# Delta attention of a four-layer block: large matrix products cut into parts between runs of small ones, token factors formed earlier, key norms by batch on column tiles of 32 tokens

## The reference

```python
def step(carry, inp):
    S, R = carry
    q_t, k_t, v_t, a_t, aR_t, b_t, g_t = inp
    kn = k_t / jnp.maximum(jnp.linalg.norm(k_t, axis=-1, keepdims=True), 1e-12)
    pred = jnp.einsum('bhji,bhj->bhi', S, kn)
    r = jnp.clip(v_t - pred, -CLIP, CLIP)
    S = a_t[..., None] * S
    kp = jnp.einsum('bhd,bhde->bhe', kn, S)
    S = S + b_t[..., None, None] * kn[..., None] * (v_t - kp)[..., None, :]
    o = jnp.einsum('bhji,bhj->bhi', S, q_t)
    R = aR_t[..., None] * R
    kpR = jnp.einsum('bhd,bhde->bhe', kn, R)
    R = R + g_t[..., None, None] * kn[..., None] * (r - kpR)[..., None, :]
    o = o + jnp.einsum('bhji,bhj->bhi', R, q_t)
    return ((S, R), o)
_, os = jax.lax.scan(step, (S0, S0), xs)
out = jnp.moveaxis(os, 0, 1).reshape(Bs, Ts, DI) @ Wo.T
```

## Time and profile before

| | |
|---|---|
| time, median of 3 runs | 3724.8 us (3717.01 to 3728.99) |
| the profiled execution | 3720.78 us, its span 3719.0 us |
| PE busy | 3255.9 us, 88% of the span, 62854 matmuls |
| DVE busy | 2569.9 us, 69% |
| ACT, POOL busy | 1383.9 us, 37%; 951.1 us, 26% |
| granted clock of TensorE, mean | 0.94 |

### The profile page before, as it was taken

The page is one execution under the profiler, slowest core; times in us unless marked ns, Lnnn a source line. Parts: engine busy times, 40 slices in busy tenths (PEclk is TensorE's granted clock), DMA queues, the critical chain, the costliest instruction groups (busy, mean ns, idle before and its releaser), DMA issues. The chain is left out here.

```text
span 3719.0 us, 141826 instructions
## 1 busy us (share of the span) xinstructions
PE 3255.9 (88%) x62854; PEld 2466.6 (66%) x62854; DVE 2569.9 (69%) x5676; ACT 1383.9 (37%) x3203; POOL 951.1 (26%) x1051
## 2 busy tenths in 40 slices
PE   7775999997799999998999999989999999848888
PEld 4564999996566666766676676666666766535555
DVE  6873111111788788878887887778878888828887
ACT  2221222222345444444444444445444444421111
POOL 2343222221222322232222223222322232211110
PEclk9886999998899999999999999999999999979998
DMA  2116666673000000000000000000000000010000
GB/s 68 53 49 223 182 187 188 185 250 90 8 8 7 12 8 8 10 10 8 7 10 9 8 7 10 9 8 7 11 9 8 8 12 6 5 46 16 23 23 13
DMA packets 98174, 168.17 MB, mean 45 GB/s; under 512 B 15400, under 2 KB 71976, under 8 KB 97312
## 3 DMA queue, kind: packets, MB, share of 16 engines
q1 hardware_dynamic: 76976, 136.07, 11.0%
q0 software_dynamic: 19440, 21.97, 4.2%
q10 hardware_dynamic: 1152, 1.06, 0.1%
HBM read 118.86 MB, written 38.09 MB: 42 GB/s over the span
## 5 line engine op out<-in xcount | busy, mean ns | idle before, releaser
L1066 POOL TENSOR_TENSOR da_M<-da_M,da_decay 128x512 f32<-128x512 f32 x256 | 269.4, 1075 | 732.5 <-DVE da_prev_end L1178 408.6
L1373 ACT COPY da_Ub<-da_U 32x256 f32<-32x256 f32 x1024 | 412.1, 402 | 17.1
L1203 DVE TENSOR_TENSOR da_eGn<-da_eGn,da_z 128x30 f32<-128x30 f32 (+14 forms) x960 | 352.1, 367 | 32.9
L1202 DVE TENSOR_TENSOR da_z<-da_eGn 128x30 f32<-128x30 f32 (+14 forms) x960 | 344.2, 359 | 27.6
L1668 PE MATMUL da_C<-da_Ub,da_Km 128*64 128x256 f32 x2048 | 298.9, 411 | 3.8 <-issue 1.6
L840 PEld LDWEIGHTS le_ps_qkv<-le_scr,le_up 128*128 128x128 f32 x2272 | 265.9, 193 | 4.8 <-ACT le_scr L670 1.8
L840 PE MATMUL le_ps_qkv<-le_scr,le_up 128*128 128x128 f32 x2272 | 267.9, 277 | 1.2 <-ACT le_scr L670 1.2
L1499 PE MATMUL da_unit<-early_buffer,da_xnT 128*128 128x512 f32 x512 | 259.2, 630 | 5.5 <-ACT da_xnT L1319 2.3
L1506 PE MATMUL da_unit<-da_xnT,early_buffer 128*128 128x128 f32 x2048 | 247.1, 277 | 9.9 <-ACT da_eGn L1358 9.9
L1506 PEld LDWEIGHTS da_unit<-da_xnT,early_buffer 128*128 128x128 f32 x2048 | 238.2, 192 | 19.0 <-ACT da_eGn L1358 17.4
L1226 DVE TENSOR_TENSOR da_M<-da_C,da_M 128x512 f32<-128x512 f32 x256 | 176.2, 688 | 72.5 <-PE da_C L1668 68.6
(11 more groups left out here) (299 smaller groups left out, 7057.1 us busy)
## 6 DMA issues: line engine op xcount, KB each, us to landing
le_up<-in_upT SPq DMA_DIRECT2D x71, 1024.0 KB, 5.1
le_scr<-moe_slots SPq DMA_DIRECT2D x71, 129.0 KB, 4.3
le_down<-in_downT SPq DMA_DIRECT2D x8, 1024.0 KB, 12.1
early_buffer<-in_x SPq DMA_DIRECT2D x16, 256.0 KB, 4.0
moe_acc<-le_y SPq DMA_DIRECT2D x32, 128.0 KB, 2.3
da_x<-moe_acc SPq DMA_DIRECT2D x128, 32.0 KB, 1.8
stream<-da_xz SPq DMA_DIRECT2D x128, 32.0 KB, 1.6
stream<-da_y POOLq DMA_DIRECT2D x128, 32.0 KB, 3.0
```

What stands on the lines that cost most here:

```text
L1066: ins = nc.gpsimd.tensor_tensor(st_, st_, decay[:, par, rec, 2 * g:2 * g + 2].rearrange("p a b -> p (a b)").unsqueeze(2).to_broadcast([P, ...
L1202: c.link(tt(t, Xm[:, s + 1:C, s:s + 1].to_broadcast([P, below, s]), Xm[:, s:s + 1, 0:s].to_broadcast([P, below, s]), ALU.mult))
L1203: c.link(tt(Xm[:, s + 1:C, 0:s], Xm[:, s + 1:C, 0:s], t, ALU.add))
L1373: ins = nc.scalar.copy(Ub[rows_of(b), :, :, b, :], U[rows_of(b), rec])
```

## The change

On PE, `rates`, `values` and `result` get an argument for a part, and `period` sets the parts apart, with small products between them. `result` of chunk i - 1, which stood between the two halves of `queries`, now stands in four parts around the last two `gram` products and `solve` of group 2. The norms of the keys, per head pair one matmul of 128 columns of weights, become four with 32 columns each, one per batch, and go in two halves ahead of and behind `state_outputs` of group 0. `turn_x` moves ahead of `state_rows`, `state_outputs` of group 1 ahead of `solve`. On DVE, the factor products come earlier, and `clipped` of groups 1 and 2 and the parts of the substitution stand otherwise. A semaphore `rows_read` is new: DVE may overwrite the factors of the first head half once PE's `state_outputs` of group 1 has read them. Banks and waits follow. The number of matmuls rises by 24 per period, all of them in the norms. The diff, cut:

```diff
-        RATE_BANK = (0, 2, 1, 2)
+        RATE_BANK = (0, 2, 0, 0)
...
-        OUT_BANK = (2, 0, 0, 0)
-        BANKS, GRAMS = ((1, 2), (0, 1), (1, 2), (0, 1)), (2, 3, 0, 1)
+        OUT_BANK = (2, 2, 2, 0)
+        KEY_BANK = (1, 0, 2, 0)
+        BANKS, GRAMS = ((1, 2), (0, 1), (1, 2), (1, 2)), (2, 3, 0, 1)
...
+                if half == 0:
+                    need(dve, rows_read, n)
...
-                if state:
-                    clipped(i, par, 2)
-                if prepare:
                     gram_out(n, pn, 1)
                     triangle_in(n, pn)
                 if state:
+                    clipped(i, par, 2)
                     update(i, 2, 0)
...
                     solved(i, 2, 0)
+                if put:
+                    result(i - 1)
+                if state:
                     turned_outputs(i, 0)
...
                 bank, cols = un[:, RATE_BANK[u]], slice((u % 2) * 512, (u % 2 + 1) * 512)
-                for kk in range(KD):
-                    ins = mm(bank, xnT[:, par, kk, :], wx[:, kk, u // 2, cols], start=(kk == 0), stop=(kk == KD - 1))
-                ins.then_inc(a_psum, 1)
+                ins = mm(bank, xnT[:, par, kk, :], wx[:, kk, u // 2, cols], start=(kk == 0), stop=(kk == KD - 1))
+                if kk == KD - 1:
+                    ins.then_inc(a_psum, 1)
...
-                for hp in range(NHP):
-                    ins = mm(un[:, 1, 2 * hp:2 * hp + 2], sq[:, hp, :], sel[:], start=True, stop=True)
-                ins.then_inc(n_psum, 1)
+                for hp in range(half * HB, (half + 1) * HB):
+                    for b in range(B):
+                        ins = mm(un[rows_of(b), 1, 2 * hp:2 * hp + 2], sq[:, hp, rows_of(b)], sel[:], start=True, stop=True)
+                if half == 1:
+                    ins.then_inc(n_psum, 1)
...
-            def result(i):
-                need(pe, oT_ready, (i + 1) * NG)
-                if exists(i + 1):
-                    need(pe, km_ready, once(i + 1, 3))
-                for hp in range(NHP):
+            def result(i, part):
+                if part == 0:
+                    need(pe, oT_ready, (i + 1) * NG)
+                    if exists(i + 2):
+                        need(pe, gram_done, once(i + 2, 1))
+                    elif exists(i + 1):
+                        need(pe, km_ready, once(i + 1, 3))
+                for hp in (2 * part, 2 * part + 1):
...
                     state_rows(i, par, 2)
-                    state_update(i, 1, 1)
+                if put:
+                    result(i - 1, 0)
+                if prepare:
+                    gram(n, pn, 0)
+                if put:
+                    result(i - 1, 1)
+                if state:
                     state_predicted(i, par, 2)
+                if prepare:
+                    gram(n, pn, 1)
+                if put:
+                    result(i - 1, 2)
+                if state:
                     solve(i, 2, 0)
                     state_outputs(i, par, 2)
-                if prepare:
-                    gram(n, pn, 0)
+                if put:
+                    result(i - 1, 3)
                 if state:
                     inner_predicted(i, par, 2)
```

## The result

The changed kernel takes 3789.0 us (median of 4 runs, 3777.95 to 3799.67) against 3720.9 for the kernel before beside it: a ratio of 1.0187, interval 1.0137 to 1.0238. It is slower by nearly 2%, 70 us from the forecast of 3719 and outside the range. The profiled execution took 3777.95 us.

A forecast was written before the change was run, and what follows sets the result against it. PE was taken to bound stage one of each period (to the last `gram`'s end), DVE stage two. Per period, -3.5 + 4.0 - 0.5 = 0.0 us over 31 periods gave 3719 us, range 3640 to 3770.

The forecast's parts named there:

- At 0.7 us lost for each shared us: +2.8.: Stage two: POOL's `rescale` of groups 0 and 1, late behind `put_out`, slows DVE's substitution by 2.8 us per period.
- 4.0 (all of it): Stage two: upper bound on DVE's loss beside POOL's `rescale`, 4.0 us per period, all the shared time.
- exclusion for whole instructions: Stage two: VectorE with two SBUF inputs and GpSimd exclude each other; loss 4.0, sum 1.2 us per period worse; not adopted.
- 1.7 - 0.4 + 0.2 - 0.3 = 1.2: Stage two on DVE: `clipped` moved +1.7, earlier lateness -0.4, wait for `inner_predicted` +0.2, fewer short waits -0.3.
- Forecast with the clock -4.0: Stage one: -3.5 us per period from PE's work, supply and hand-over, with -0.5 for the clock.
- (b): Stage one, PE: norms in 32-column tiles take 0.46 us per half, 0.92 for 1.88, so -0.96 per period.
- rival 2: Norms' weights load one after another, deciding from 0.64 us per half; 30 us more, 3749 us; chance 0.20.
- (c): Stage one, PE: halts for instruction supply in pieces of 128 matmuls fall from 5.3 to 2.6 us, -2.7 per period.
- the check in the prediction: Stage one before: work without halts 28.5 and halts 5.3 make 33.8 us, against 33.91 measured.
- (d): Stage one: after `gram` of group 2, DVE's mask product and `clipped` take 2.7 us, PE's filling work 2.5; +0.2.
- -0.5: Clock: half of the 1.0 us between mean and chosen period comes back, -0.5 us per period, bounds 0 and -1.0.
- Rivals 1 and 3: Rival 1: POOL costs nothing, 3637 us, chance 0.22; rival 3: halts move, their sum stays, 3803 us, chance 0.06.

The follow-up runs named there:

- E3: Kernel before, with POOL's `rescale` of groups 0 to 2 held until DVE's `update` of group 2; 3806.2 us, ratio 1.0252.
- E6: E1 with POOL's `rescale` of groups 0 and 1 held until DVE's `update` of group 2; 3760.9 us, ratio 1.0102.
- E8: E1 with `norms_of_keys` in the form and place of the kernel before; 3705.9 us, ratio 0.9959.
- E1: Changed kernel with POOL's `rescale` of groups 0 and 1 moved ahead of `put_out`; 3666.5 us, ratio 0.9877.
- E4: Kernel before with only the norms of the keys on 32-column tiles, in one piece; 3699.0 us, ratio 0.9975.
- E2: Changed kernel with `result` back in one piece between the two halves of `queries`; 3658.2 us, ratio 0.9854.
- E7: E1 with the `rates` of stage one whole again, at their first halves' place, ahead of a `solve`; 3689.3 us, ratio 0.9926.
- E10: E2 with four unread products around the third `gram`, where the changed kernel has parts of `result`; 3664.1 us, ratio 0.9827.
- E5: E1 with four unread products filling PE's idle time ahead of the period's first `solve`; 3633.0 us, ratio 0.9757.
- E12: E6 with the unread products of E5 in PE's idle time at the period's end; 3733.0 us, ratio 1.0032.
- E11: E5 with two more unread products between the first half of the norms and `state_outputs`; 3625.3 us, ratio 0.9729.

## Why the prediction was wrong

**The step that failed: "At 0.7 us lost for each shared us: +2.8."** The mechanism was named, with its place and its order of events, and its price was too low. The substitution lost 4.8 us per period (26.53 against 21.73), 4.6 of it in its first step. The other 2.0 us over 30 periods are 60 us, and with them 3719 becomes 3779, against 3778.0 for the profiled execution. The price came from a row of POOL starting from idle, and for such a start it was about right: 3.1 us in E3 (24.82 - 21.73) and in E6 (25.01 - 21.93). It doesn't hold straight behind `put_out`. The bound above, "4.0 (all of it)", was too low too: DVE's step stood still from 1768.37 us, 0.9 us before the last issue ended, with POOL's first `rescale` already begun by its record (1768.14). The sentence on the Trainium skill ("SBUF — State Buffer", section "SBUF: two separate sides"), exclusion for whole instructions, was nearer to the changed kernel than 0.7 was; E6 lies between. What isn't settled is what closed the gap between POOL's instructions: the issues ahead, or that POOL's first instruction already stood in its queue when DVE's first step came up. E6 changed both; it shows only that issues with no instruction ready behind them cost DVE nothing.

**The rest of stage two** came as put: without the substitution it grew by 1.33 us, forecast 1.7 - 0.4 + 0.2 - 0.3 = 1.2. `clipped` of group 2 brought 1.34 us of it (1.71 from 1766.06 to 1767.77, less the 0.37 that stood behind the last `gram` before), as forecast. Its wait for `inner_predicted` was 0.89 us in the period shown and 0.45 in the mean of the 29, against 0.2; the short waits that fell away make up for it.

**Stage one.** Forecast with the clock -4.0, measured -4.02 (35.08 to 31.06). That it is so close is in part luck, since parts that were off in both directions cancel: (b) the norms take 0.36 us a half, 0.72 for 1.88 or -1.16 in place of -0.96, and rival 2 is out, which wanted 0.64 or more: a record takes 11 ns, where a quarter of one with 128 columns (1.88 us for 16) would be 29. What the term is worth in the time is less sure. With the old norms E8 is 0.8% slower than E1 by the ratios, 30 us, but of its 1.3 us per period only 0.5 stand without low clock; alone in the kernel before it gave 0.3 (E4), since halts and a wait of `growth` took the rest. (c) Halts fell by 2.4 us per period, forecast 2.7. The level was put too high, 5.3 against 4.0 before; the check in the prediction could not hold, since PE's 29.43 us of 33.91 leave 4.48 for all its idle time. The cause was partly wrong: `result` in its parts carries most of it (E2: 3.3 without them), the halves of `rates` do not (E7). How the parts do it stays open in part, as unread products at two of the four places took only 0.6 away (E10). What the halves do, to cover two hand-overs in place of one, the prediction missed; it counted them only as +0.2. (d) The hand-over at `clipped` is there and small: 8.5 us in 13 waits for DVE's L1224, 0.3 per period against 0.2.

**The clock.** "-0.5" in stage one was -0.3: without low clock the stage went from 34.26 to 30.50 us, so 3.76 of the 4.02 are work and halts. That PE would wait ahead of the next period and lose the clock there was seen, and in the changed kernel it cost little. It cost 2.1 us per period as soon as the collision was gone (E1: 32.09 against 29.95 in its six periods without low clock).

Rivals 1 and 3 are out by the same rows. The range ended at 3770, and neither the forecast's own span, which took POOL's loss up to 3.5, nor a rival had it higher.

## What to carry to other kernels

Where a transfer's issue on GpSimd waits for a product, look at what stands behind it in GpSimd's order before that product is moved: here four instructions of `rescale` behind `put_out` cost 3.1% (1.0187 against 0.9877), and moving two calls ahead of it took that back. A price read where an engine starts from idle isn't the price where its instructions come queued up. In a run of small matmuls a large product can be mostly free (E10: 1.2 of 1.8 us), and cut in two it covers two hand-overs; but look at the clock behind idle time of TensorE that stands ahead of such a run: here filling it made the program 1.2% faster (E1 to E5, by the ratios).

## What the runs showed of the hardware

- A VectorE step of 0.19 us on two SBUF inputs took 4.01 us while GpSimd finished four transfer issues and ran three instructions of about 1 us; where GpSimd started from idle, VectorE got one step in between each two of its instructions, at 0.97 to 1.04 us a step. Four transfer issues with no instruction ready behind them left its steps at their length (0.27 us on 108 elements, E6).
- 32 records with weights of 32 columns on four column tiles, which share all rows, took 0.36 us; 16 with 128 columns take 1.95. The Trainium skill ("TensorE: Matmul & The Clock Gate", Part 3, what overlaps) would let a weight load run beside a matmul only where row groups differ; here the measurement, 11 ns a record, speaks against it.
- The idle time ahead of the first `solve` goes with the clock behind it. In the five runs with 1.8 to 1.9 us of idle time the clock was below 1.00 for 4.7 to 8.1 us of stage one; in the five with 0.3 us or less and the new norms in halves, E2, E5 and E10 to E12, for 0 to 2.2 us. The changed kernel lies between in idle time, at 1.35, with 2.0 us. Idle time isn't all of it: six of E1's 29 periods kept the clock, and the kernel before, E3 and E4 lost it for 1.6 to 3.4 us with 0.3 or less.
- Unread products made the program faster: E11 does 2.7 us more on PE per period than E1 and is 1.5% faster by the ratios.
